# Late scatters in a graph network kernel: waiting for each batch of eight ahead of the next one

## The reference

```python
src = jax.random.randint(key2, (100000,), 0, 6250, jnp.int32)
dst = jnp.minimum((6250 * jax.random.uniform(key3, (100000,)) ** 2.0).astype(jnp.int32), 49999)

def _sage_conv(h, src, dst, Wl, bl, Wr, num_nodes):   # four of these, two per layer
    agg = _mean_aggr(h, src, dst, num_nodes)          # mean of h[src] over the edges into each node
    return agg @ Wl.T + bl + h @ Wr.T
```

## Time and profile before

| what | value |
|---|---|
| time, median of 3 runs | 4441.4 us (4439.45 to 4443.1) |
| span of the profiled execution, first to last instruction | 5171.8 us |
| time of the profiled execution outside its span | not given |
| PE busy | 3159.9 us, 61% |
| DVE busy | 2679.3 us, 52% |
| POOL busy | 2510.8 us, 49% |
| late scatters (L857), 390 of them | 395.5 us busy, 127.8 us idle before them |

### The profile page before, as it was taken

The page is one execution under the profiler, slowest core; times in us unless marked ns, Lnnn a source line. Parts: engine busy times, 40 slices in busy tenths (PEclk is TensorE's granted clock), DMA queues, the critical chain, the costliest instruction groups (busy, mean ns, idle before and its releaser), DMA issues.

```text
span 5171.8 us, 61853 instructions
## 1 busy us (share of the span) xinstructions
PE 3159.9 (61%) x18737; PEld 2317.1 (45%) x18737; DVE 2679.3 (52%) x5868; ACT 1560.3 (30%) x3684; POOL 2510.8 (49%) x2587
## 2 busy tenths in 40 slices
PE   1555555554755555555555554111159999999999
PEld 0333333333534344344344333100047777788777
DVE  4888888888645555555555556300001254433333
ACT  1777777776222222222222222100000011111000
POOL 7666666664666666666666666777720000000000
PEclk9999999999986667667667666555579999999999
DMA  5555555555134444444444443100037666666776
GB/s 183 192 198 191 195 194 194 192 192 164 56 98 111 112 121 111 116 117 111 114 118 112 111 118 85 58 0 0 13 126 282 215 218 245 247 248 251 259 276 228
DMA packets 387596, 797.88 MB, mean 154 GB/s; under 512 B 207412, under 2 KB 264600, under 8 KB 361128
## 3 DMA queue, kind: packets, MB, share of 16 engines
q1 hardware_dynamic: 239330, 586.35, 33.9%
q0 software_dynamic: 82320, 90.28, 7.9%
q10 hardware_dynamic: 65718, 118.62, 6.2%
HBM read 581.03 MB, written 213.92 MB: 154 GB/s over the span
## 4 chain that ended last, share of the span: by engine, by line
PE 25%; issue 23%; SPq 19%; DVE 3%; another core or an unknown queue 1%; DMA 0%; ACTq 0%; ACT 0%; DVEq 0%; POOL 0%
PE ps L1181 18%; SPq L626 14%; PE ps L1111 6%; SPq L601 1%; SPq L596 1%; SPq L622 1%; SPq L607 1%; SPq L617 1%; PE ps L1064 1%; ACTq L64 0%; DMA area<-adj 0%; PE ps L1083 0%; PE ps L1056 0%; DVE second L1650 0%
## 5 line engine op out<-in xcount | busy, mean ns | idle before, releaser
L770 POOL DMA_INDIRECT area<-src_table,early x784 | 752.5, 960 | 469.6 <-remote 225.5
L770 POOL DMA_INDIRECT area<-relu_table,early x784 | 739.6, 943 | 421.3 <-issue 212.4
L953 PE MATMUL ps<-ident,area 96*128 96x96 f32 x2352 | 441.4, 356 | 804.3 <-issue 555.4
L953 PEld LDWEIGHTS ps<-ident,area 96*128 96x128 f32 x2352 | 355.2, 213 | 939.2 <-issue 782.4
L1181 PE MATMUL ps<-second,area 128*128 128x288 bf16 x5194 | 652.1, 286 | 0.2 <-DVE second L1823 0.2
L1682 DVE TENSOR_TENSOR_SCAN area<-flags,area,ps 96x512 f32<-96x512 int8 x196 | 250.0, 1276 | 647.6 <-issue 552.0
L1181 PEld LDWEIGHTS ps<-second,area 128*128 128x128 f16 x5194 | 509.0, 98 | 128.5 <-DVE second L1823 0.5
L1650 DVE SCALAR_TENSOR_TENSOR second<-second,area,ps 128x512 bf16<-128x512 f32 x784 | 538.1, 741 | 0.0
L857 POOL DMA_INDIRECT adj<-out_ring x390 | 395.5, 1014 | 127.8 <-issue 127.8
L781 POOL DMA_INDIRECT adj<-copies_ring,cell_ring x392 | 388.6, 991 | 125.6 <-issue 118.9
L1111 PE MATMUL ps<-early,area 128*128 128x288 bf16 x2401 | 322.0, 292 | 204.9 <-issue 204.9
(11 more groups left out here) (330 smaller groups left out, 4709.0 us busy)
## 6 DMA issues: line engine op xcount, KB each, us to landing
area<-adj SPq DMA_DIRECT2D x147, 1632.0 KB
area<-adj SPq DMA_DIRECT2D x55, 1568.0 KB
adj<-early SPq DMA_DIRECT2D x102, 816.0 KB
soft_sums<-out_ring ACTq DMA_DIRECT2D x196, 384.0 KB
second<-key_dram SPq DMA_DIRECT2D x98, 512.0 KB
area<-dst_table SPq DMA_DIRECT2D x784, 48.0 KB
sums<-out_ring ACTq DMA_DIRECT2D x196, 192.0 KB
second<-caps_dram SPq DMA_DIRECT2D x98, 192.0 KB
```

The costliest lines, as they stand in the source:

```text
L770: pool.indirect_dma_start(out=src_rows[:, s, c, :], out_offset=None, in_=gather_table[p], in_offset=bass.IndirectOffsetOnAxis(ap=src_cols[ ...
L953: last = nc.tensor.transpose(ps[:, b, c * F:(c + 1) * F], r[:, (s * CH + c) * P:(s * CH + c + 1) * P], ident[0:F, 0:F])
```

## The change

`batch_done` is called with the batch just issued, right behind its scatters, in place of with the batch before it. The call behind the loop goes away, since the last batch is now announced in the loop.

```diff
                                 out=adj_all, out_offset=bass.IndirectOffsetOnAxis(ap=cell_late[:, c:c + 1], axis=0),
                                 in_=copies_late[:, c:c + 1], in_offset=None).then_inc(late_made[i % 2], 16)
-                        if i:
-                            batch_done(i - 1)
-                    batch_done(BATCHES - 1)
+                        batch_done(i)
```

## The result

The new kernel takes 4540.0 us (4538.1 to 4540.5) against 4442.2 us before (median of four runs): ratio 1.0226, 95% interval 1.0214 to 1.0238, so +98 us. The forecast was 4540 us.

What follows compares the result with a forecast made beforehand. The prediction took POOL's late scatters, overlapped by PE's first-convolution jobs, to bound the stage. Terms of 0 + 82 + 17 = +99 us on 4441.4 gave 4540 us; range 4480 to 4600.

Steps and rivals of the forecast that it cites:

- POOL sets the end in the timed runs: Late scatter loop: first-convolution jobs overlap the scatters, and POOL finishes last, at 523 us against PE's 346.
- Part 1: Announcements on POOL's queue: moving them forward in code gains 0 us; events already come 1.2 us behind their own batch.
- Part 2: POOL empty at 48 batch boundaries: 1.7 us each, 82 us in all (43 to 121).
- Part 3: Landings of late scatters that meet a fill now delay POOL: 17 us (0 to 35).
- The new profile's span: Whole profiled execution of the new kernel: 5171.8 + 82 + 5, about 5259 us.
- (a): Late loop: POOL's pauses let slowed PE run, near 4441 us at break-even, down to 4258 us; chance 0.05.
- (b): Late loop: each batch end meets a fill, about 2 us more per landing, 178 us, 4619 us; chance 0.11.
- (c): PE ends later than POOL and hides the change: 4441 us, or up to +43 if partial; chance 0.04 each.

Runs made afterwards that it cites:

- Old order with sixteen: Kernel before with BATCH = 16 in place of 8, each batch still announced behind the next one's scatters: 4447.3 us, ratio 1.0003.
- the lag of two: Kernel before with the wait for batch i moved behind batch i+2, using three late_made semaphores: 4440.8 us against 4446.3 us, ratio 0.999.
- two of eight scatters: Only two of each batch's eight late scatters sent, six left out, in both orders: old order 4253.2 us, new order 4252.9 us.

## Why the prediction was right, point by point

- **POOL sets the end in the timed runs.** Right, and read from a profile that showed the opposite. The argument that 2775, 844 and 1060 us don't fit into 4441 held: in the undistorted profile the stage from the first late scatter to the reduced joint rows takes about 539 us (2835.5 to 3374.4), not 844. The 606 us that the prediction left for it were too many: the first late scatter starts at 2835.5 us, 60 us later than the 2775 priced for POOL alone. PE waits for POOL from job 20 on (forecast: tile 21): DVE's reductions are 6.00 us apart up to job 19 at 3005.8 us and irregular from 3021.9 us.
- **Part 1, nothing gained by announcing earlier in the code.** Right. In the second profile the first batch's event is at 2848.7, again 1.2 us behind the batch; beside fills events come up to 6.3 us late, at no cost. Old order with sixteen is the same in time as the kernel before, and the lag of two costs nothing.
- **Part 2, 48 x 1.7 us.** Right: the gap is 1.97 us, 1.67 us more than 0.30, 80 us in all. Both pieces were measured where the forecast took them from: 1.2 us to the event, 0.8 us from there to the next scatter. By the Trainium skill's 2.0 us ("DMA: Bandwidth & Descriptors", Anatomy of one DMA) it would have been an estimated 1.5 us and 74 us in all; the measured 1.67 us decides.
- **Part 3, 17 us beside fills.** Right in size, 19.6 us (99.8 - 80.2), and roughly in place. The gap behind batch 1 is 5.86 us, 3.9 us over the plain one (forecast 5); behind batches 4 to 8 it is 2.6 to 7.1 us, 14 us over the plain one together (forecast 12 us over batches 5 to 14). PE set the pace until 2991 us, the end of batch 10, not 14, and batches 9 and 10 met no fill; those five that met one waited 2.9 us more on average, where I had put in 2 us at a chance of two in three for nine batches. Fewer meetings, each longer, made nearly the same sum.
- **Sum.** +99 us forecast, +98 us measured. That it is this close is partly luck: part 2 was 2 us too high and part 3 was 2.6 us too low, and inside part 3 two errors offset each other. The tail was taken as unchanged and is: 32.9 us from the end of the last scatter to the reduction of the second joint row, then 32.8 us. In it the last landing came 2 us later, and a shorter fill and last job made up for that.
- **The new profile's span, 5259 us forecast, 4538 us found.** Wrong. The step that failed was the assumption that the profiled execution would be slowed again as the first was. The second profile of the kernel before was not slowed either. With it the forecast of POOL's last scatter near 3875 us fell; counted from the loop's start the last scatter is at 603 us, where the forecast said 607.
- **Rivals.** (a), that pauses feed PE, is out: PE needs no feeding in runs that aren't slowed, and 59 us are lost in the very half in which PE has work queued. (b), that each batch end meets a fill, is out for batches of eight: most gaps are 1.97 us. With batches of four 42 of the 97 gaps are longer than the plain one, 55 us in all. (c), cover, is out for this kernel and real for a shorter stream: with two of eight scatters it hides all of 115 us more idle time.

## What to carry to other kernels

Here a wait on an engine's queue cost what it took to refill the engine; its place in the order of announcements cost nothing. Put the wait for a DMA behind enough further work for the queue to stay full: one batch of eight was enough here, where the queue held twelve; one batch of two was not. Price a drained queue as landing time plus restart less the gap that is there anyway, times the number of waits, and then ask if that engine ends last; if not, the price is zero. When a profiled execution is much longer than the runs, add up its stages against the runs' time before trusting which engine ends last, or take a second profile.

## What the runs showed that I had not expected

- The first profile of the kernel before was slowed by 730 us, with PE at 2.80 us a matmul beside POOL's DMAs. It was so not only in the late loop: its first late scatter starts 433 us later than in the second profile, and the stretch from there to the links is 303 us longer. None of the later profiles was slowed in this way. The cause stays open.
- One scatter of 128 two-byte elements took 8 to 10 us longer to land when 95 of its lanes wrote to neighbouring addresses (event 9.8 and 11.8 us behind it, 2.2 us with the cells spread). A change of two strides made the kernel 12 us faster.
- In the stretch in which PE waits for fills, its jobs take longer. Three of PE's rows from the kernel before (second profile), PE busy in order of time:

```profile
3301.71 6.17 PE L1111 MATMUL ps<-early,area 128*128 128x288 bf16 x49 [2.32 <-DMA area<-adj]
3311.96 8.85 PE L1111 MATMUL ps<-early,area 128*128 128x288 bf16 x49 [4.08 <-DMA area<-adj]
3321.80 6.18 PE L1111 MATMUL ps<-early,area 128*128 128x288 bf16 x49 [0.98 <-DMA area<-adj]
```

Busy by stretch, same profile, while PE sets the pace and after it:

```profile
2892.00:3006.00 114.00, 113.76 (x929) 90.62 (x927) 14.80 (x39) 0.00 (x0) 85.09 (x89) 1.00 0.65 226
3006.00:3342.00 336.00, 208.72 (x1372) 148.38 (x1372) 23.56 (x62) 0.00 (x0) 253.16 (x262) 0.79 0.42 139
```

The granted clock is 1.00 (2.4 GHz throughout) where PE is busy without a break and 0.79 on average where it is busy for 62% of the time, so part of that stretch is at 1.2 GHz. A job of 49 matmuls takes 6.2 or 8.9 us in these rows. It was no part of the sum, since both kernels have it; in the new kernel the stretch's clock is 0.74.
